# Self-attention of a perceiver block: q and k of two batches made in the cross-attention's last products, the rest as units among 16 groups

## The reference, cut to what matters

```python
# x (4, 256, 256), ctx_1024 (4, 4096, 256), all float32
x = x + cross(layernorm(x), ctx_1024)        # softmax(q k^T / 16) v, one head, out @ Wo.T + bo
x = x + self_attention(layernorm(x))
x = x + soft_moe(layernorm(x))               # 64 experts of 32 slots, phi_w (2048, 256)

def self_attention(h):                       # 16 heads of 16 columns, 256 tokens, 4 batches
    q, k, v = split(h @ c_attn_w + c_attn_b)
    attn = softmax(where(causal, q @ k.T / 4, lowest))
    attn[heads 0, 1, 2] = renormalised(attn * (1.6 on the head's third of the keys, else 1))
    return merge_heads(attn @ v) @ c_proj_w + c_proj_b

def soft_moe(h):
    logits = h @ phi_w.T + phi_b             # then softmax over slots and over experts,
    ...                                      # slot inputs, tanh(layernorm), expert products, mix
```

## Time and profile before

| | us |
|---|---|
| three timed runs | 672.75, 676.78, 682.08 (median 676.78) |
| profiled execution, its own time | 672.18 |
| span of that execution | 670.4 |
| cross-attention | 0 to 291.4 |
| self-attention | 291.4 to 417.5 |
| experts | 417.5 to 670.4 |

### The profile page before, as it was taken

How to read it: one execution, slowest core, us unless ns; L and a number is a source line. 1 busy time by engine, 2 the same in 40 slices (tenths; PEclk the granted TensorE clock), 3 DMA queues, 4 the chain that set the end, 5 groups by cost and what they waited for, 6 DMA issues and landing times. The chain is left out here.

```text
span 670.4 us, 10668 instructions
## 1 busy us (share of the span) xinstructions
PE 598.2 (89%) x3740; PEld 475.4 (71%) x3740; DVE 402.1 (60%) x794; ACT 348.1 (52%) x1047; POOL 249.6 (37%) x201
## 2 busy tenths in 40 slices
PE   5998999999999998997887867999999876769998
PEld 4887998899989987975555546555558652448887
DVE  3766566666667664336477777699995378335000
ACT  2545444444444435632787861579996366751210
POOL 1352262233223232022696770133546149155000
PEclk8999999999999999999797999999999996699999
DMA  7122012102211220019993000300006147680000
GB/s 258 64 95 94 32 65 94 64 32 82 77 65 36 93 77 0 2 58 171 196 204 127 0 1 4 124 0 0 1 1 137 51 127 236 202 254 8 17 17 23
DMA packets 41586, 53.48 MB, mean 80 GB/s; under 512 B 3649, under 2 KB 37057, under 8 KB 41409
## 3 DMA queue, kind: packets, MB, share of 16 engines
q1 hardware_dynamic: 41536, 52.84, 28.7%
HBM read 48.63 MB, written 4.19 MB: 79 GB/s over the span
## 5 line engine op out<-in xcount | busy, mean ns | idle before, releaser
L247 POOL TENSOR_TENSOR ctx_lo<-ctx_stage,ctx_hi 128x1024 fp32r<-128x1024 f32 x32 | 76.3, 2387 | 157.3 <-DVE ctx_hi L622 135.8
L637 DVE TENSOR_TENSOR pT_lo<-ps,pT_hi 128x512 fp32r<-128x512 f32 x64 | 41.2, 686 | 60.0 <-ACT pT_hi L517 60.0
L342 PE MATMUL ps<-ctx_hi,pT_hi 128*128 128x256 f32 x256 | 75.2, 294 | 1.5 <-DVE pT_lo L637 1.4
L343 PE MATMUL ps<-ctx_lo,pT_hi 128*128 128x256 f32 x256 | 72.4, 283 | 0.0
L344 PE MATMUL ps<-ctx_hi,pT_lo 128*128 128x256 f32 x256 | 72.4, 283 | 0.0
L494 ACT CAST ctxT_hi<-ps 128x512 fp32r<-128x512 f32 x64 | 34.6, 593 | 62.7 <-PE ps L299 62.5
L1688 ACT ACTIVATE comb<-comb,cneg 128x64 f32<-128x64 f32 x160 | 62.9, 401 | 0.0
L629 DVE TENSOR_SCALAR_CACHE_REDUCE scores<-ps,qbk 128x512 f32<-128x512 f32 x64 | 47.5, 750 | 21.2 <-PE ps L311 21.2
L1574 PE MATMUL pf<-phiT,h3T 128*128 128x512 f32 x128 | 60.2, 591 | 0.0
L1659 PE MATMUL pf<-phiT,comb 128*128 128x256 f32 x256 | 56.2, 379 | 0.0
L508 ACT ACTIVATE probs<-scores,negmax 128x512 f32<-128x512 f32 x64 | 46.0, 728 | 16.3 <-DVE rowsum L648 16.3
(11 more groups left out here) (204 smaller groups left out, 1368.3 us busy)
## 6 DMA issues: line engine op xcount, KB each, us to landing
ctx_stage<-in_ctx_dram SPq DMA_DIRECT2D x32, 512.0 KB, 3.3
w_more<-in_L_ffn_expert_w_dram SPq DMA_DIRECT2D x11, 1024.0 KB, 5.4
h3T<-in_L_ffn_expert_w_dram SPq DMA_DIRECT2D x5, 1024.0 KB, 5.3
qk_parts_dram<-qk_parts SPq DMA_DIRECT2D x8, 384.0 KB, 5.3
q_rows<-qk_parts_dram SPq DMA_DIRECT2D x24, 128.0 KB, 6.5
disp<-qk_parts_dram SPq DMA_DIRECT2D x24, 128.0 KB, 5.8
disp<-in_L_ffn_phi_w_dram SPq DMA_DIRECT2D x1, 2048.0 KB, 8.2
phiT<-in_L_ffn_expert_b_dram SPq DMA_DIRECT2D x4, 512.0 KB, 10.0
```

Source lines behind the costliest of these rows:

```text
L247: nc.gpsimd.tensor_tensor(ctx_lo[:, cols], ctx_in_sb[:, c % SLOTS, :], ctx_hi[:, cols].bitcast(F32), ALU.subtract).then_inc(split_g, 1)
L342: nc.tensor.matmul(pO[q][:, 0:D], pT_hi[:, c % 2, q, cols], hi, start=c == 0 and j == 0, stop=False)
L343: nc.tensor.matmul(pO[q][:, 0:D], pT_hi[:, c % 2, q, cols], lo, start=False, stop=False)
L637: nc.vector.tensor_tensor(pT_lo[:, c % 2, q, :], probs_banks(c, alone)[q][:], pT_hi[:, c % 2, q, :].bitcast(F32), ALU.subtract).then_inc(p ...
```

## The change

1. `cross_attention`: stages 0 to 3 of q and k are made in the last products. PE's `project_qk(0..3)` stand ahead of `mix(LAST, 3..6)`; ACT, DVE and POOL make the parts there, SP stores them and issues the 24 row loads before the block's end. The turnings of the norms move to c = 1, 2 and 7. The weights are scaled at c = 0. phi_b is split on a (128, 16) tile and reloaded as three rows. The first rows of q and k lie in what was the context stage (`front`) and one half of the scores (`back`).
2. `self_attention`: opens with the scores of group 0. The last batch's products, the values, stages 4 to 7 of q and k, four output projections with sums and statistics, and the turning of phi_w stand as units among 16 written-out groups; most share one bank, `psX`. The scores have three banks, one for each part. Each half of the row tiles is a tensor of its own.
3. `soft_moe`: phi is turned already, six of eight tiles have their scale; the second half of the rows is turned between logits. The bias product has 3 rows in place of 96.

The diff, cut to its core (`store_parts` and `stack_rows` do what they did before):

```diff
+            sp.dma_start(phi_cols[:], phi_b.rearrange("(p e) -> p e", p=P)).then_inc(phi_in, 16)
+            sp.wait_ge(phi_v, 2 * NPART - 1)
+            sp.dma_start(phi_dram.rearrange("c (p e) -> p c e", p=P), phi_parts[:]).then_inc(phi_out, 16)
+            sp.wait_ge(phi_out, 16)
+            sp.wait_ge(qkhi_a, DH * B)
+            sp.wait_ge(xbo_g, 1)
+            sp.dma_start(kept.phib[0:NPART, :], phi_dram).then_inc(phi_in, 16)
+            for s in range(0, 4, 2):
+                for k in (s, s + 1):
+                    store_parts(sp, kept, qk_dram, parts(k), k)
+                if s == 0:
+                    sp.wait_ge(split_g, NCH * B)
+                for k in (s, s + 1):
+                    stack_rows(sp, kept, qk_dram, q_rows, k_rows, k)
+            sp.wait_ge(phi_in, 32)
 
...
+            pool.wait_ge(w2_in, W2_IN)
+            projection_bias(0, QT * (LAST - 1))
+            second_scale(LAST - 1)
+            for s in range(4):
+                pool.wait_ge(middle_a, s + 1)
+                nc.gpsimd.tensor_tensor(parts(s)[:, 2, :], rest(s), parts(s)[:, 1, :], ALU.subtract).then_inc(low_g, 1)
+            projection_bias(QT * (LAST - 1), QT * LAST)
...
+            def project_qk(s):
+                rows, tokens_of = qk_stage(s)
+                pe.wait_ge(h2T_a, 2)
+                pe.wait_ge(wq_a, 2)
+                at_least(pe, rest_v, s - 1)
+                for c in range(DH):
+                    last = nc.tensor.matmul(pS[s % 2][:], kept.w_qkv[:, c, rows * P:(rows + 1) * P], h2T[:, c, tokens_of],
+                                            start=c == 0, stop=c == DH - 1)
+                last.then_inc(qk2_mm, 1)
...
-                if c in H2T_AT:
-                    if c == 3:
-                        pe.wait_ge(xadd_v, QT * LAST)
-                    if c == 6:
-                        pe.wait_ge(h2T_a, 1)
-                    transpose_second(H2T_AT[c], pS[c % 2])
+                    transpose_second(0, pS[0])
+                if c == 2:
+                    pe.wait_ge(xadd_v, QT * LAST)
+                    transpose_second(1, pS[1])
+                if c in QK_AT:
+                    project_qk(QK_AT[c])
+                if c == NCH - 1:
+                    pe.wait_ge(rest_v, 3)
+                    transpose_second(2, pS[0])
...
+                    act.wait_ge(w2_in, W2_IN)
+                    nc.scalar.activation(kept.w_qkv[:, :, 0:D], kept.w_qkv[:, :, 0:D], ACT.Identity, scale=ATT_SCALE).then_inc(wq_a, 1)
+                    nc.scalar.activation(kept.b_qk[:, 0:DH], kept.b_qk[:, 0:DH], ACT.Identity, scale=ATT_SCALE).then_inc(wq_a, 1)
+                if c == 1:
+                    second_turned(0, pS[0])
+                if c == 2:
+                    second_turned(1, pS[1])
                 if c < NCH - 2:
                     exps(LAST, c + 2)
-            act.wait_ge(w2_in, W2_IN)
-            nc.scalar.activation(kept.w_qkv[:, :, 0:D], kept.w_qkv[:, :, 0:D], ACT.Identity, scale=ATT_SCALE)
-            nc.scalar.activation(kept.b_qk[:, 0:DH], kept.b_qk[:, 0:DH], ACT.Identity, scale=ATT_SCALE)
+                if c in QK_AT:
+                    high_part(QK_AT[c])
+                if c - 1 in QK_AT:
+                    middle_part(QK_AT[c - 1])
+            second_turned(2, pS[0])
...
+                if c == 0:
+                    focus_factor(dve, nc, kept, ident)
+                    phi_bias_parts()
                 if c == 1:
                     add_product(LAST - 1, pS[1])
                     second_statistics(LAST - 1)
+                if c == 2:
+                    dve.wait_ge(split_g, NCH * B)
+                    query_extras(nc, kept, q_rows)
+                if c == 3:
+                    dve.wait_ge(exp_a, QT * NCH * LAST + 2 * QT)
+                    key_extras(nc, kept, k_rows)
+                    second_norm(LAST - 1)
                 if c == 4:
-                    second_norm(LAST - 1)
+                    key_focus(dve, nc, kept, k_rows, 0)
+                if c in QK_AT:
+                    rest_of(QK_AT[c])
             invert_sums(LAST)
...
+            for s in (4, 6):
+                for k in (s, s + 1):
+                    store_parts(sp, kept, qk_dram, parts[:, k - 4, :, :], k)
+                for k in (s, s + 1):
+                    stack_rows(sp, kept, qk_dram, q_late, k_late, k)
+            sp.dma_start(phi_nat, phi_w.rearrange("(k p) d -> p k d", p=P)).then_inc(phi_in, 16)
             sp.wait_ge(phi_in, 16)
...
+            for i in range(GROUPS):
+                b, g = i // NG, i % NG
+                if i + 1 < GROUPS:
+                    normalise(i + 1)
+                if i == 0:
+                    pad_values(0, 1)
+                if i == 1:
+                    low_part(4)
+                    pool.wait_ge(h_v, TT + QT * B)
+                    nc.gpsimd.tensor_tensor(x_sb[:, QT * LAST:TT, :], x_sb[:, QT * LAST:TT, :],
+                                            b_proj[:].unsqueeze(1).broadcast_to([P, QT, D]), ALU.add).then_inc(xb_g, 1)
+                if i == 2:
+                    low_part(5)
+                    low_part(6)
+                if i == 3:
+                    low_part(7)
+                if g == 1 and b:
+                    pool.wait_ge(av_mm, NG * b)
+                    pad_values(b, 1)
+                if g == 3 and b < LAST:
+                    pool.wait_ge(av_mm, NG * b + NG // 2)
+                    pool.wait_ge(values_v, b + 2)
+                    pad_values(b + 1, 0)
+                if g == 3 and b:
+                    output_scale(b - 1)
+                if i == 4:
+                    nc.gpsimd.memset(ones[0:NPART, :], 1.0).then_inc(const_g, 1)
...
-        psS, psT, psO = bank[0:4], bank[4:7], bank[7]
+        psS, psX, psT, psO = bank[0:3], bank[3], bank[4:7], bank[7]
+        V_BANK = (3, 5, 7, 3)
...
+            def project_out(b):
+                pe.wait_ge(o_a, DH * (b + 1))
+                for q in range(QT):
+                    t = QT * b + q
+                    for c in range(DH):
+                        last = nc.tensor.matmul(psX[:, q * D:(q + 1) * D], oT[:, c, t * P:(t + 1) * P], w_proj[:, c, :],
+                                                start=c == 0, stop=c == 1)
+                last.then_inc(out_mm, 1)
...
+            for s in range(2):
+                pe.wait_ge(rows_in[s], 16 * STACK)
+            for part in range(3):
+                score(0, part)
             transpose_attended()
             product_of_norm()
+            for s in range(3):
+                project_v(s)
+            score(1, 0)
             product_of_attended()
+            score(1, 1)
+            score(1, 2)
             for s in (2, 3):
                 pe.wait_ge(rows_in[s], 16 * STACK)
-            pe.wait_ge(rest_v, 7)
+            score(2, 0)
+            for i in range(GROUPS):
+                if i + 2 < GROUPS:
+                    score(i + 2, 1)
+                    score(i + 2, 2)
+                if i == 0:
+                    pe.wait_ge(attT_a, B)
+                    pe.wait_ge(values_v, 2)
+                    pe.wait_ge(xadd_v, QT * B)
+                transpose(i)
+                if i == 1:
+                    pe.wait_ge(h2T_a, B)
+                    project_qk(4)
+                if i == 2:
+                    pe.wait_ge(rest_v, 6)
+                    project_qk(6)
+                if i == 3:
+                    pe.wait_ge(rest_v, 8)
+                    project_v(3)
+                if i == 9:
+                    pe.wait_ge(phi_in, 16)
+                    pe.wait_ge(out_v, 1)
+                    transpose_phi(0)
+                if i in (11, 12, 13):
+                    pe.wait_ge(phi_a, i - 9)
+                    transpose_phi(2 * i - 20)
+                if i + 3 < GROUPS:
+                    if i == 5:
+                        for s in (4, 5):
                             pe.wait_ge(rows_in[s], 16 * STACK)
+                        pe.wait_ge(frows_v, 10)
+                    if i == 7:
+                        for s in (6, 7):
+                            pe.wait_ge(rows_in[s], 16 * STACK)
+                    score(i + 3, 0)
+                if i == 1:
+                    pe.wait_ge(values_v, 3)
+                if i:
+                    mix(i - 1)
+                if i == 0:
+                    transpose_second()
+                if i in (1, 2):
+                    pe.wait_ge(rest_v, 2 * i + 3)
+                    project_qk(2 * i + 3)
+                if i == 5:
+                    pe.wait_ge(values_v, 4)
+                    project_out(0)
+                if i == 9:
+                    pe.wait_ge(phi_a, 1)
+                    project_out(1)
+                if i == 10:
+                    pe.wait_ge(out_v, 2)
+                    transpose_phi(1)
+                if i in (11, 12):
+                    pe.wait_ge(phi_v, i - 10)
+                    transpose_phi(2 * i - 19)
+                if i == 13:
```

(153 more changed lines are left out.)

717 lines of the change are left out of this document (293 added, 424 removed).

## The result

| | before | after |
|---|---|---|
| median of the runs | 676.2 us (672.8 to 682.1, 4 runs) | 703.3 us (701.1 to 703.4, 4 runs) |
| profiled execution, span | 672.2, 670.4 us | 701.1, 699.4 us |
| mean granted clock | 0.964 | 0.949 |

The ratio is 1.038, 95% interval 1.031 to 1.046: slower. I had said 679.0 and 662 to 693, and given "slower" a chance of 0.2, so the time lies outside the range. Of the 29.0 us by which the span grew, my steps gave 5.3.

A forecast was written before the change was run, and what follows sets the result against it. PE bounds the last cross-attention products; in self-attention groups no engine is full, a ring of DVE maxima, ACT exponentials and DVE copies sets 4.19 us. Terms sum to +5.3: 672.2 + 5.3 + 1.5 = 679.0 us, range 662 to 693.

The forecast's parts named there:

- A: End of the first block: comes later, at 309.8, held by SP's chain of stores and row stacks; +18.4 us.
- B: Self-attention block's start to the first group's copy: 21.5 us where it was 42.9; -21.4 us.
- E: End of the second block, after the last copy: shorter than the 13.2 us before; -6.4 us.
- F: Start of the experts: shorter, with two turnings between logits and half clock counted; -0.9 us.
- C: Groups 0 to 4 of self-attention: four woven projections at 3.0 us each above plain periods of 4.2; +7.9 us.
- D: Groups 4 to 15 of self-attention: added sums, phi turnings and waits for late rows, less a subtraction and loop cost; +7.7 us.
- third rival: Self-attention: late rows decide, PE stands over 9 us at group 5, group 7 waits 5 more; 693 us, chance 0.15.
- The weave hides: Self-attention groups: woven parts fit in the engines' slack, the late-row wait goes too; 667.6 us, chance 0.25.
- Stores land in 2.6 us: First block's end: SP is not last, the block ends at 304 though rows are ahead; 673.2 us, chance 0.15.
- The border costs SyncE nothing: First block's end: issues are released ahead, self-attention's start waits for rows alone, 302; 671 us, chance 0.05.
- The likeliest case: Whole kernel: the forecast itself, 679.0 us, own range 673 to 687, chance 0.40.

The follow-up runs named there:

- run 1: Changed kernel with the product of the slots' biases back on 96 rows, rows 3 to 95 zero: 693.3 us, ratio 1.023.
- run 3: Kernel before with only the bias product's rows changed, 3 instead of 96: 684.7 us, ratio 1.011.
- run 4: Changed kernel with the row loads of stages 2 and 3 issued at the start of the self-attention block: 695.0 us, ratio 1.026.
- run 8: Changed kernel with the stores of stages 2 to 7 issued by GpSimd on its own queue, row loads still on SyncE's: 696.2 us in one run.
- Run 7: Run 6 with the pieces of stages 4 to 7 left out altogether (products, parts, stores, row loads): 680.9 us, ratio 1.004.
- Run 6: Changed kernel without waits for the rows of stages 4 to 7, and phi_w's load issued first in the self-attention block: 694.5 us, ratio 1.027.
- run 5: Changed kernel, scores of groups 8 to 15 from the first two batches' key rows, no late-row waits before the groups' end: 704.6 us in one run.
- run 2: Changed kernel with the bias product on 3, 96, 32, 64, 128, 3, 96 and 16 rows, four units each: 696.6 us in one run.
- run 10: Changed kernel with 96-row bias product, stage 2 and 3 row loads moved to self-attention, phi_w's load behind them, GpSimd issuing stores 4 to 7: 681.5 us, ratio 1.007.
- run 12: Run 10 with all stores by GpSimd, stack 1 also in the second block, value tiles ahead of the first scores: 681.3 us, ratio 1.006.

## Why the prediction was wrong, step by step

**The direction and the frame held.** SyncE was the last to reach the border, the idle gap and the clock of 0.50 in it were there, and the start of self-attention got 21 us shorter. A, B and E alone would give -4.3 us measured, against my -9.4.

**F is the step that failed.** I priced the start of the experts only and never compared the logits' own instructions, so the bias product on 3 rows stood in my sum at nothing. The start did come out 2.2 us shorter (4.7 from the block's end to the first product, 6.9 before), but 32 bias products at 0.30 cost 9.6, the two turnings between units 0.9 (two periods of 2.67 instead of 2.23), and the half clock in the first unit 1.5 (its four products took 3.46 us, 1.98 in the next unit). Sum +9.8, measured +9.1. Runs 1 and 3 show the bias term alone from both sides: 8.9 and 9.0 us in the profiles, 10.0 and 7.7 in the medians. Without it the time is 693.3, still just above my range: F is 10.0 of the 23.7 us by which the span missed my sum, and A, C and D are 13.1.

**A was mis-sized by 4.5 us, in two terms.** Stores 2 and 3 were issued at 297.6 and not at 295.4, since stage 1's low part ended at 291.2 and not at 289, and both stacks stand behind its store. About 2.2 us of this lie in the execution and not in the change. The same instruction of DVE, ahead of the last products, before and then after:

```profile
245.22 1.29 DVE L637 TENSOR_TENSOR pT_lo<-ps,pT_hi 128x512 fp32r<-128x512 f32 x2 [1.81 <-ACT pT_hi L517]
```

```profile
247.43 1.29 DVE L790 TENSOR_TENSOR pT_lo<-ps,pT_hi 128x512 fp32r<-128x512 f32 x2 [1.81 <-ACT pT_hi L653]
```

In run 4, whose edit comes later, it starts at 245.51. The second term is the chain's own: the stores landed in 10.0 and 10.3 us where I had 8.2, and the two stacks behind took 6.3 instead of 5.9. (My 1.5 MB of rows at 127 GB/s take 12 us and not 11; the sum doesn't use this.) Of my two reasons, full DMA engines and the queue's order, run 8 supports the first: with the queue changed a store still takes 9.7 us. I had cited the Trainium skill (DMA: Bandwidth & Descriptors, "Queues, rings and completion order") for the ring's order. The same section says that a completion's semaphore write lands only after every earlier write of that DMA engine, across its queues; run 8 agrees with this, and the order within one ring isn't needed for it. Nor was the whole of A on the path: run 4 brought the border 16.0 us forward and gained 8.3, because the rows are needed next.

**C was mis-sized by 3.3 us.** I gave each woven stage 3.0 us, 12 for four, above periods of 4.2. Run 7 shows the plain periods at 4.8 (19.3 for four) and the four stages at 12.2 in all. So the stages' price was right in sum (it came as periods of 12.7 and 9.3 us in groups 1 and 2, where I had named 10 and 9), and the base was too low: I had taken four periods of 4.2 (16.8). The lost 2.5 us lie in groups 0 and 3, 5.20 and 5.43 us long even without stages; they hold the memsets and the value product that I had put inside the 12. That these are the cause was not tried.

**D was mis-sized by 5.3 us, mostly in the waits.** Run 6 has 53.4 us with the units in and the waits out, so the units cost 4.3 over before, where I had 2.7 net of waits, and the waits cost 8.7, where I had 5.0 for late rows and clock. The first wait, at group 5, was about as forecast: 2.7 us for 3.5, with the rows 62.7 us after the block's start (I had 58.6, though my terms add up to 58.8 with the quickest store and 61.5 with a usual one) and TensorE there at 60.0 (54.6). The term that failed is the one for the last rows at group 7: 4.2 us where I had 0.5. The remaining 1.8 go with the clock (0.79 granted from 368 to 395, 1.00 over the same groups in run 6), where I had 1. This is the second half of my third rival, "group 7 waits 5 more"; its first half, over 9 us at group 5, did not come. I had put its chance at 0.15 because four stages have the queue for themselves. What I missed: SyncE waits for stage 5's low part before it issues stage 4's rows (9.09 us at 352.60), store 6 lands 10.2 us after its issue behind 12 row loads, and rows move at 121 GB/s (window 370 to 375), a rate at which the 3.1 MB of 24 loads take 26 us.

**The other rivals.** The weave hides (0.25): no, 12.2 us in groups 0 to 4. Stores land in 2.6 us (0.15): only with no rows ahead. The border costs SyncE nothing (0.05): no, run 4. The likeliest case had the right mechanisms with three of them too small, and one missing.

## What to carry to other kernels

When operands are repacked, compare the shapes of the products that use them, instruction by instruction, in stages the change seems to leave alone: here a product with fewer rows was dearer than one padded with zeros, 0.30 us at a time. When transfers are moved ahead, ask what else stands on the same DMA engines and which waits the issuing engine takes between them; moving an issue to another queue frees the issuing engine, but does not make packets in flight go away, and the new queue can be slower to start. And a wait on a queue hides the next on it: price the queue's whole list, since removing the first alone (run 5) gains nothing.

## What the hardware showed that I had not expected

- A bf16 weight load and product of 3, 16, 32 or 64 rows between products of 128 rows takes 0.30 us more per unit than one of 96 or 128 rows (3.10 against 2.80, run 2), though load and product have the same durations (0.09 and 0.38 us). The gap stands ahead of the small load. What makes the step was not tried further.
- A store of 384 KB takes 2.6 to 3.1 us alone on SyncE's queue and 4.0 to 4.8 alone on GpSimd's (runs 8, 10 and 12), but 9.7 there with 12 row loads in flight on SyncE's (run 8).
- An idle border costs twice: in the empty window 307.6 to 314 TensorE's clock was at the lower level, 1.2 GHz (0.50), and the mean over the next 6 us of work was 0.60; after 3.7 us of idle time ahead of the experts the first unit's four products took 3.46 us (0.55 granted from 441.6 to 445.5), 1.98 in the next.
